# Layers phase of a two-branch attention kernel: inverse roots of the norms once per batch, half the key remainders, second scores in row blocks, and a rewoven order

## The reference, cut to what matters

```python
def _layer(x, wqkv, qs, ksc, wo, lg, lb, w1, b1, w2, b2):
    h = shift_token(x)
    q, k, v = split(h @ wqkv)                    # 8 heads of 64
    q = l2norm(q) * qs;  k = l2norm(k) * ksc     # one norm for each token and head
    q, k = rotary_xpos(q, k)
    o = local_attention(q, k, v)                 # windows of 128, each looks one window back
    x = x + o @ wo
    h = layernorm(shift_token(x)) * lg + lb
    a, g = split(h @ w1 + b1)                    # hidden size 682
    return x + (a * gelu(g)) @ w2 + b2
```

## Time and profile before

| | us |
|---|---|
| time, median of 3 runs | 4979.3 (4978.19 to 4979.38) |
| span of the profiled execution | 4976.4 |
| layers phase in it, from the first transposes to the end | 1421 to 4976 |
| PE, DVE, ACT, POOL busy | 4105.8, 3737.6, 2470.1, 1445.1 |

### The profile page before, as it was taken

One profiled execution on the slowest core, in us unless ns is written; L12 is line 12 of the kernel. 1 busy time (PEld: TensorE's weight loads), 2 busy tenths in 40 slices (PEclk: granted clock), 3 DMA queues, 4 the chain that ended last, 5 costly groups with the idle time before them and its releaser, 6 DMA issues.

```text
span 4976.4 us, 86488 instructions
## 1 busy us (share of the span) xinstructions
PE 4105.8 (83%) x30816; PEld 2420.5 (49%) x30816; DVE 3737.6 (75%) x6579; ACT 2470.1 (50%) x2841; POOL 1445.1 (29%) x1467
## 2 busy tenths in 40 slices
...
GB/s 27 22 18 23 19 23 18 23 18 22 10 57 16 20 29 19 19 23 24 23 25 19 19 27 15 68 16 12 19 27 20 28 19 19 26 20 24 24 19 19
DMA packets 122499, 114.37 MB, mean 23 GB/s; under 512 B 9372, under 2 KB 121040, under 8 KB 122320
## 3 DMA queue, kind: packets, MB, share of 16 engines
...
...
## 4 chain that ended last, share of the span: by engine, by line
issue 24%; PE 20%; POOL 13%; DVE 12%; ACT 2%; SPq 0%; DMA 0%; POOLq 0%; DVEq 0%
PE f_p L979 4%; POOL f_hT_l L1362 4%; DVE f_rn L233 3%; POOL f_u L1350 3%; POOL f_u L1347 3%; PE f_p L1015 3%; PE f_p L990 2%; PE f_p L925 2%; DVE f_bt L1216 2%; DVE f_ss L1206 2%; PE f_p L1037 1%; PE f_p L998 1%; PE f_p L965 1%; PE f_p L966 1%; PE f_p L909 1%
## 5 line engine op out<-in xcount | busy, mean ns | idle before, releaser
L652 DVE TENSOR_REDUCE m_negm<-m_p 128x2 f16<-128x1024 f32 x512 | 602.1, 1225 | 159.5 <-PE m_p L438 157.9
L540 ACT ACTIVATE m_Pr<-m_p 128x1024 f32<-128x1024 f32 x512 | 497.3, 1020 | 228.7 <-PE m_p L454 222.7
L1347 POOL TENSOR_TENSOR f_u<-f_u,f_bt 128x1024 f32<-128x1024 f32 x128 | 300.5, 2348 | 933.9 <-DVE f_bt L1216 933.9
L1236 DVE TENSOR_REDUCE f_negm<-f_p 128x4 bf16<-128x1024 f32 x256 | 297.4, 1225 | 194.4 <-PE f_p L947 193.4
L694 POOL TENSOR_TENSOR m_rc<-m_rc,m_rs 128x512 f32<-128x512 f32 x64 | 84.9, 1326 | 1189.6 <-DVE m_rs L617 1189.6
L1037 PE MATMUL f_p<-f_xhT_h,f_w_h 128*128 128x512 f16 (+1 forms) x768 | 325.7, 424 | 70.6 <-DVE f_hp L1307 70.6
L438 PE MATMUL m_p<-m_KT,m_QT 128*128 128x512 f16 x1024 | 281.2, 382 | 65.8 <-DVE m_negm L652 29.5
L454 PE MATMUL m_p<-m_QT,m_KT 128*128 128x512 f16 x1024 | 276.8, 382 | 58.3 <-DVE m_negm L652 33.0
L1362 POOL TENSOR_TENSOR f_hT_l<-f_hp,f_hT_h 128x512 f16<-128x512 f32 x192 | 235.5, 1227 | 304.3 <-ACT f_hp L1135 304.2
L1350 POOL TENSOR_TENSOR f_u<-f_u,f_rn 128x1024 f32<-128x1024 f32 x128 | 249.4, 1949 | 256.0 <-DVE f_rn L237 256.0
L1037 PE MATMUL f_p<-f_xhT_h,f_w_l 128*128 128x512 f16 (+1 forms) x768 | 323.2, 421 | 0.0
(11 more groups left out here) (233 smaller groups left out, 10587.5 us busy)
## 6 DMA issues: line engine op xcount, KB each, us to landing
...
```

What stands on the lines that cost most here:

```text
L540: act.activation(Pr[kt % 2][:, 2 * u:2 * u + 2, :].rearrange("p h t -> p (h t)"), psum[w.slot("M2", g, kt, u)][:, :], ACT.Exp).then_inc(*w ...
L652: dve.tensor_reduce(negm[:, 2 * u:2 * u + 2, h], psum[w.slot("M1", h, u)][:, :].rearrange("p (a k) -> p a k", a=2), AX.X, ALU.max, negate= ...
L1236: dve.tensor_reduce(negm[:, :, h], psum[w.slot("L1", h)][:, :].rearrange("p (n k) -> p n k", n=NT), AX.X, ALU.max, negate=True).then_inc(* ...
L1347: pool.tensor_tensor(u[r][:], u[r][:], bt[:], ALU.add).then_inc(*bt_used.up(I))
```

## The change

Four things change in `layers_phase`.

1. QK,t no longer makes the inverse roots. The sums of squares of all four tiles go into one tensor (`ss`, 128x64), and a new step **RN** after QK,3 makes all inverse roots at once. POOL's scaling becomes a step of its own, **NM,t**, after RN. u has four buffers instead of two.
2. k's remainder is written once (`klt`, no second copy); ST,t transposes 4 blocks of it instead of 8, and ACT brings back half as much. For this q's high part lies in the first half of the partitions for even heads and in the second for odd ones.
3. L2 works on a pair of heads. The maxima are copied four times side by side (new DVE step in **LM**, before PE's transposes), so that the subtraction is made by matmuls that use 32 rows each; k's remainder uses 64 rows of each head. All waiting for two slots stands ahead of the pair, and ACT's two exponents follow each other.
4. The spreading of the reciprocal (X) moves from DVE to ACT, and the order string is rewoven.

The order string (the first two of its five rows, each way):

```diff
-    order = """A.XT F.W1,0 A.QK,0 F.W1,1 A.XR F.H1,0 A.SQ,0 A.QK,1 A.HI,0 F.W1,2 A.SQ,1 A.SH,0 F.H1,1 N.LX A.QK,2 A.HI,1
-               A.ST,0 F.H1,2 F.W1,3 A.SH,1 A.SQ,2 A.QK,3 A.HI,2 A.ST,1 F.H1,3 F.W1,4 A.SQ,3 F.W1,5 F.W2,0 F.W2,1 F.H1,4
+    order = """A.XT F.W1,0 A.QK,0 F.W1,1 A.XR F.H1,0 A.QK,1 F.W1,2 F.H1,1 N.LX A.QK,2 F.W1,3 F.H1,2 A.QK,3 A.RN F.H1,3
+               F.W1,4 A.NM,0 A.HI,0 A.SQ,0 A.SH,0 F.W1,5 A.NM,1 A.HI,1 A.SQ,1 A.SH,1 F.W2,0 F.H1,4 A.ST,0 F.W2,1 A.NM,2 A.HI,2
```

```diff
             def l2(I, hp):
+                w.wait(w.is_drained("LM"), w.is_free("L2", 2 * hp))
+                pe.wait_ge(*w.is_free("L2", 2 * hp + 1))
...
+                for j0 in range(2):
+                    for e in range(2):
+                        for j in (j0, j0 + 2):
+                            g = slice((2 * e + j // 2) * G32, (2 * e + j // 2 + 1) * G32)
+                            pe.matmul(dst(e, j), sel[g, 2 * hp + e, :], mT[g, q(j)], start=(j0 == 0), stop=False, skip_group_check=True)
+                for e in range(2):
+                    h = 2 * hp + e
+                    for j in range(NT):
+                        pe.matmul(dst(e, j), KH[:, h, j * W:(j + 1) * W], QT[:, h, q(j)], start=False, stop=False, skip_group_check=True)
                 for j in range(NT):
-                    pe.matmul(dst, sel[:, h, :], mT[:, q], start=True, stop=False, skip_group_check=True)
-                    pe.matmul(dst, KH[:, h, j * W:(j + 1) * W], QT[:, h, q], start=False, stop=False, skip_group_check=True)
-                    mm = pe.matmul(dst, KL[:, h, j * W:(j + 1) * W], QT[:, h, q], start=False, stop=True, skip_group_check=True)
+                    for e in range(2):
+                        half = slice(e * HALF, (e + 1) * HALF)
+                        mm = pe.matmul(dst(e, j), KL[half, hp, j * W:(j + 1) * W], QT[half, 2 * hp + e, q(j)], start=False, stop=True,
+                                       skip_group_check=True)
...
+            def rn_(I):
+                dve.wait_ge(*ss_ready.at(I, NT))
+                link(dve.tensor_scalar(flat(ss), flat(ss), (NORM_MIN * WSCALE) ** 2, None, ALU.max))
+                rsqrt(dve, link, flat(ss), flat(rn), flat(rt))
+                dve.memset(mark_v[:], 0.0).then_inc(*rn_ready.up(I))
...
+            def lm(I):
+                dve.wait_ge(*w.is_drained("L1", H - 1))
+                dve.tensor_copy(negm4[:, :, :, 0:H], negm[:].unsqueeze(2).to_broadcast([P, NT, P // G32, H])).then_inc(*negm_ready.up(I))
...
+            def rd(I, hp):
+                act.wait_ge(*rden_ready.at(I, hp + 1))
+                act.activation(X[hp % 2][:], rden[hp % 2][:].unsqueeze(3).to_broadcast([P, NT, 2, DH]), ACT.Copy).then_inc(*x_ready.up(I))
...
+            def nm(I, t):
+                pool.wait_ge(*bt_used.at(I, t + 1))
+                pool.wait_ge(*rn_ready.at(I, 1))
+                pool.tensor_tensor(u[t][:].rearrange("p (h d) -> p h d", d=DH), u[t][:].rearrange("p (h d) -> p h d", d=DH),
+                                   rn[:, t, :].unsqueeze(2).to_broadcast([P, 2 * H, DH]), ALU.mult).then_inc(*u_ready.up(I))
```

More of the change, by code:

```diff
@@ L748, in layers_phase @@
     NK = 2 * (NT - 1) * W + W
+    G32 = 32
+    HALF = P // 2
     base_cos, base_sin = xpos_tables(T, DH, W, 8.0)
@@ L788, in tiles_of @@
             "LM": lambda: [(("LM",), "pair", 1)],
-            "L2": lambda: [(("L2", *r), "pair", 1)],
+            "L2": lambda: [(("L2", 2 * r[0] + e), "pair", 1) for e in range(2)],
             "PV": lambda: [(("PV", *r), "pair", 1)],
@@ L930, in st @@
                 r = t % 2
-                for key, ready, parts in (("STa", q_lo_ready, (qst, khh)), ("STb", stack_ready, (kll,))):
+                for key, ready, parts in (("STa", q_lo_ready, (qst, khh)), ("STb", stack_ready, (klt,))):
                     pe.wait_ge(*ready.at(I, t + 1))
@@ L935, in st @@
                     for i, m in enumerate(parts):
-                        for h in range(H):
-                            mm = pe.transpose(ps[:, (i * H + h) * P:(i * H + h + 1) * P], m[r][:, h, :], ident[:])
+                        for h in range(H if key == "STa" else NP_):
+                            src = m[r][:, h, :] if key == "STa" else m[r][:, h * P:(h + 1) * P]
+                            mm = pe.transpose(ps[:, (i * H + h) * P:(i * H + h + 1) * P], src, ident[:])
                     mm.then_inc(*w.fills(key, t))
```

145 lines of the change are left out of this document (74 added, 71 removed).

## The result

| | before | after |
|---|---|---|
| time, median, us | 4978.7 (4973.99 to 4979.38) | 5231.5 (5224.03 to 5239.09) |
| span of the profiled execution, us | 4976.4 | 5235.9 |
| mean granted clock, share of 2.4 GHz | 0.938 | 0.901 |
| PE, DVE, ACT, POOL busy, us | 4105.8, 3737.6, 2470.1, 1445.1 | 4092.8, 3020.3, 2470.4, 1461.7 |

The changed kernel is slower: ratio 1.0509, 95% interval 1.0494 to 1.0524, or +253 us. I had forecast +171 (5150, range 5060 to 5225). DVE lost 717 us of work, a fifth of what it had, and the kernel got longer all the same. PE has 512 matmuls fewer and is hardly less busy, since more of them ran at the lower level of its clock (1.2 GHz).

A forecast was written before the change was run, and what follows sets the result against it. No engine is full; a chain between engines bounds the turn, with PE sharing the bound in its last part. 28 x (2.0 + 1.65 + 2.7) = 178, less 8, gave +170 on 4976.4: 5146, stated as 5150, range 5060 to 5225.

The forecast's parts named there:

- RN, and the serial tiles behind it: W1,0 to L1,0: all four tiles run serially behind RN, remainders colliding, 5.4 us a tile; +2.0 us a turn.
- The copy behind W2,2's sum, +1.65: L1 to the maxima: DVE's copy for LM stands behind W2,2's sum, delaying everything to the turn's end; +1.65 us.
- Row blocks: Second scores: a pair of heads takes 1.6 us instead of 2.3, bounds 1.4 and 2.3.
- X on ACT ahead of exponents 6 and 7, +1.55: PV,0 to PV,3: exponents 6 and 7 stand behind X in ACT's queue, so PV,3 comes 1.55 us later.
- (c): From PV,0: third pair, exponents, XH, its remainder and X delay head 7's mask; PV,3 at 18.7 instead of 17.16, +1.55.
- The end of the turn, +0.7: After PV,3: the last pair's X moves to ACT ahead of OL,2, delaying OL,2, RX,3's product and OL,3; +0.7 us.
- It doesn't reach the end, for three reasons: Maxima to next W1,0: PE's 2.8 us less work a turn doesn't shorten this part; together +2.7 us.
- (a): Maxima to PV,0: the first exponent waits for a whole pair, 2.6 us after the maxima's copy instead of 2.14; +0.45.
- (b): After PV,0: no scores fill PE's queue while ACT copies; PV,1 comes at 4.6, just as before.
- rival C: Second scores and PE's new holes: row blocks don't overlap or the clock falls; 5215 us or more, chance 0.12.
- DVE's work on a tile: W1,0 to L1,0: about 3.65 us plus 0.75 for W1's product, less than PE's 6.5, so PE sets the pace.
- the rule for two SBUF inputs: Inverse root before the change: two-input DVE operations contend with GpSimd's SBUF reads, so its 2.36 us wait for POOL.

The follow-up runs named there:

- filled kernels: PE's holes filled with idle matmuls whose results nobody reads: the kernel before so filled took 4957.6 us, the changed kernel (last filling) 5094.5 us.
- the plan's number: Changed kernel with maxima copy early, scalings ahead, X on DVE, pairs behind PV; then XH's slot counted 1.5 places earlier in the PSUM plan: 4930.2 us.

## Why the prediction was right and wrong

- *RN, and the serial tiles behind it:* right. NM,0 at 35.6, period 5.2, L1,0 at 61.7 against 35.4, 5.4 and 61.8. The remainders collide in all four tiles, as I took it, at 1.66 us each instead of 1.83. But I compared it with one turn of before that reached L1,0 in 59.8; the mean of the 28 is 60.49, since some reach it in 61.5. The term was +1.2.
- *The copy behind W2,2's sum, +1.65:* right as a chain; the filled kernels differ there by 1.74. What came on top, 1.0, is the first scores at the lower level.
- *Row blocks:* a pair is 1.7 us (I took 1.6), and without blocks 2.3.
- *X on ACT ahead of exponents 6 and 7, +1.55:* size right (+1.40), cause right in part. PV,3 waits for head 7's mask in every turn, as chain (c) has it, and comes 18.56 behind PV,0 where PV,0 runs at the upper level (forecast 18.7). But 1.02 of the 1.40 lies ahead of PV,2, in the first half of (c): third pair, exponents 4 and 5, XH, its remainder, a slot. X's engine changed nothing there (9.00 on either), moving the pairs took 2.75 out (6.25). The other 0.38 lies where X is, and whether X on ACT makes it stays open, since X on DVE met POOL.
- *The end of the turn, +0.7:* too small, +1.43. X on ACT is 0.52 of it (run with X on DVE), and 0.90 is W1,0's wait for the output projection's slot (run with the plan's number), which I had not looked up in the order: RX,3's slot was W1,0's before.
- **The step that failed** is "It doesn't reach the end, for three reasons", (a) and (b), with the sum built on it: what PE does from LM on was taken at the upper level, the first scores were taken to run just as before, and (b) said PV,1 would come "just as before". PE's new holes pulled the granted clock down for L1, the first pair and PV,0: 4.8 us a turn in after (115.67 - 110.89), 0.6 before. I had this as half of rival C, with a price for the pairs alone and none for L1 and PV. That C's 5215 comes nearest is luck: it is made of pairs of 2.3 us, and a pair takes 1.7. The chains came to 5.6 a turn where I had 6.35, and the clock adds 4.2, together 9.8.
- *Smaller slips:* DVE's work on a tile comes to 3.80 by its own terms (3.65 - 1.05 + 1.2), not 3.65, which is still less than PE's 6.5. And the rule for two SBUF inputs that I quoted doesn't cover L233, which reads one tensor (f_rn<-f_rt); the row shows only that it took 2.36 us beside POOL's L1347.

Not settled: which hole pulls the clock down for which group. The fillings show that together they do. They show too that a lower clock lengthens PE's own groups behind L1,0 and, with the scalings ahead, the path up to it.
